# A two-layer graph attention kernel: paired head sums, a two-partition row scan and an extra PE product

## The reference, cut to what matters

```
# layer 0
score = einsum('ehd,ehd->eh', K[src], Q[dst]) / sqrt(32) + edge_bias
m     = segment_max(score, dst)
ex    = exp(score - m[dst]);  denom = segment_sum(ex, dst)
out   = segment_sum(ex / denom[dst] * V[src], dst) @ Wp + bp
# then residual, layer norm, 1024-wide GELU network, layer norm
# layer 1
feat  = (h @ W_lin + b_lin) @ W_gat
e     = leaky_relu(sum(feat*attn_l)[src] + sum(feat*attn_r)[dst], 0.2)
m     = segment_max(e, dst); a = exp(e - m[dst]) / segment_sum(...)
out   = leaky_relu(segment_sum(feat[src] * a, dst) + gat_bias, 0.01) + h_in
```

## Time and profile before

| | |
|---|---|
| time, 3 runs | median 5992.57 us (5990.07 to 6003.05) |
| profiled execution | 5990.54 us, of which the span is 5988.6 |
| busy in the span | PE 91%, PEld 72%, DVE 82%, POOL 63%, ACT 53% |
| mean granted PE clock | 0.896 of 2.4 GHz |
| gathers of layer 0 | start at 369.2, last at 2648.5 us |
| gathers of layer 1 | start at 3660.1, last at 5734.3 us |
| longest shares of the chain that ended last | PE L816 35%, issue 18%, DVE L1199 7%, DVE L1193 7% |

### The profile page before, as it was taken

One profiled execution on the slowest core, in us unless ns is written; L12 is line 12 of the kernel. 1 busy time (PEld: TensorE's weight loads), 2 busy tenths in 40 slices (PEclk: granted clock), 3 DMA queues, 4 the chain that ended last, 5 costly groups with the idle time before them and its releaser, 6 DMA issues.

```text
span 5988.6 us, 127287 instructions
## 1 busy us (share of the span) xinstructions
PE 5460.7 (91%) x26094; PEld 4327.4 (72%) x26094; DVE 4924.3 (82%) x12464; ACT 3152.8 (53%) x10275; POOL 3747.5 (63%) x4022
## 2 busy tenths in 40 slices
PE   8978888888888888888999998999999999999988
PEld 5556666666666666667999996777777777777766
DVE  4469999999999999996777775887888788878864
ACT  3446666666566566643333334555555555655533
POOL 1147776666667666644444446777777777777733
PEclk9999999999999999999999997777777777767789
DMA  5668898888888888872222224777777777777767
GB/s 177 212 222 290 286 290 284 286 287 282 287 283 288 286 284 283 288 234 83 85 85 85 84 83 140 221 218 222 218 220 218 219 218 218 220 218 219 218 201 230
DMA packets 723026, 1313.61 MB, mean 219 GB/s; under 512 B 109088, under 2 KB 502132, under 8 KB 722421
## 3 DMA queue, kind: packets, MB, share of 16 engines
q0 software_dynamic: 200192, 634.41, 36.8%
q1 hardware_dynamic: 444802, 422.18, 23.4%
q10 hardware_dynamic: 77426, 250.73, 10.9%
HBM read 964.16 MB, written 342.73 MB: 218 GB/s over the span
## 4 chain that ended last, share of the span: by engine, by line
PE 37%; DVE 30%; issue 18%; POOL 5%; DMA 4%; DVEq 3%; SPq 2%; ACT 2%; POOLq 1%; ACTq 0%
PE bank L816 35%; DVE sred L1199 7%; DVE prod L1193 7%; DVE ev L1284 5%; DVE acc L1299 4%; POOL Gf L525 3%; DMA Gf<-ft_tab,srcs 3%; PE bank L819 2%; POOL Gf L576 1%; DVE U L1251 1%; DVE Y L1252 1%; DVE scan L1261 1%; DVEq L1181 1%; DVEq L1284 1%; DVE scan L1239 1%
## 5 line engine op out<-in xcount | busy, mean ns | idle before, releaser
L816 PE MATMUL bank<-ev,oh 128*128 128x264 f32 x7040 | 2310.6, 459 | 88.7 <-DVE ev L1284 88.0
L525 POOL DMA_INDIRECT Gf<-kv_tab,srcs x1564 | 1570.4, 1004 | 724.1 <-issue 480.1
L525 POOL DMA_INDIRECT Gf<-ft_tab,srcs x1564 | 1598.9, 1022 | 483.2 <-issue 401.8
L816 PEld LDWEIGHTS bank<-ev,oh 128*128 128x128 f32 x7040 | 1480.0, 223 | 346.0 <-DVE ev L1284 123.4
L816 PE MATMUL bank<-Gf 128*128 128x128 f32 (+3 forms) x6480 | 1263.8, 346 | 22.1 <-ACT Gf L805 15.6
L1284 DVE TENSOR_TENSOR ev<-Gf,ex 128x528 f32<-128x528 f32 x1760 | 1232.9, 701 | 2.1 <-ACT ex L688 1.4
L816 PE MATMUL bank<-qs,oht 128*128 128x256 f32 x3520 | 954.8, 394 | 226.9 <-DVE prod L1193 226.6
L816 PEld LDWEIGHTS bank<-Gf 128*128 128x128 f32 x6480 | 967.2, 192 | 221.0 <-issue 98.5
L621 ACT ACTIVATE absd<-lane,dlocs 128x128 f32<-128x128 f32 x3520 | 1112.9, 389 | 4.0 <-DVE bms L1166 3.5
L816 PEld LDWEIGHTS bank<-qs,oht 128*128 128x128 f32 x3520 | 599.5, 190 | 437.6 <-issue 371.8
L1299 DVE SCALAR_TENSOR_TENSOR acc<-acc,same,bank 128x264 f32<-128x264 f32 x1540 | 736.0, 478 | 34.2 <-PE bank L816 30.8
...
## 6 DMA issues: line engine op xcount, KB each, us to landing
...
qs<-q_tab SPq DMA_DIRECT2D x880, 128.0 KB
qs<-dst_tab SPq DMA_DIRECT2D x880, 128.0 KB
Gf<-sums SPq DMA_DIRECT2D x196, 132.0 KB, 2.1
...
Gf<-in_x SPq DMA_DIRECT2D x196, 128.0 KB, 2.1
Gf<-kv_tab,srcs POOLq DMA_INDIRECT x1564
Gf<-ft_tab,srcs POOLq DMA_INDIRECT x1564
```

The costliest lines, as they stand in the source:

```text
L525: pool.indirect_dma_start(out=rows[layer][:, m % SLOTS[layer], k, :], out_offset=None, in_=tab, in_offset=bass.IndirectOffsetOnAxis(ap=src ...
L816: return nc.tensor.matmul(o, a, r, start=first, stop=end)
```

## The change

1. **Row stage.** Two partitions hold the two directions: partition 0 the row in forward order, partition 1 reversed. PE makes them by products with `ident` and a reversed identity `anti` (four products of 2x128 for three transposes of 1x128). ACT copies two rows for three, DVE makes one scan `uy` over 2x136 for two scans and a subtraction. `columns` becomes four products: two of 8 columns, which yield the difference of both directions on all partitions (with constants `minus_first` and `plus_second`), and two of one column. PE's `rexp` product goes; ACT's `rescale` moves from s=2 to s=4 and works on 128 partitions.
2. **Layer 0, head sums.** `reduce` runs on odd steps only, over two steps at once (128x1024 in, 128x32 out); `prod` has four places for two.
3. **Layer 1, PE.** Every step has one further product of 128x256 in fp32 (`unread`), into a PSUM bank that nothing reads, between `spread` and `agg`.

Left out of the diff: the tiles' memsets and constants in the prologue (each engine waits for two more of POOL's).

```diff
@@ -189,26 +189,29 @@
         oh0 = sb("oh0", [P, 2, 2])
-        prod = sb("prod", [P, 2, 2, D])
+        prod = sb("prod", [P, 4, 2, D])
         absd = sb("absd", [P, 2, 4, P])
...
         ats = sb("ats", [P, P + 1])
-        wa = sb("wa", [P, 1])
+        wa = sb("wa", [P, 3])
         sred = sb("sred", [P, P])
...
         S = sb("S", [P, P])
-        scan1 = sb("scan1", [P, P])
-        scan2 = sb("scan2", [P, P + 1])
-        wlf = sb("wlf", [1, 3, H * RW + 1])
-        U = sb("U", [1, H * RW + 1])
-        Y = sb("Y", [1, H * RW + 1])
-        ct = sb("ct", [1, H])
-        xy = sb("xy", [1, 2, P])
-        rx = sb("rx", [1, H])
-        rexp = sb("rexp", [1, H])
+        scan1_0 = sb("scan1", [P, P + 1])
+        scan1, last_0 = scan1_0[:, 0:P], scan1_0[:, P - 1:P + 1]
+        scan2_0 = sb("scan2", [P, P + 2])
+        scan2, first_0 = scan2_0[:, 1:P + 2], scan2_0[:, 0:2]
+        anti = sb("anti", [P, P])
+        minus_first = sb("minus_first", [2, P])
+        plus_second = sb("plus_second", [2, P])
+        wv = sb("wv", [2, 2, H * RW + 1])
+        uy = sb("uy", [2, H * RW])
+        xy = sb("xy", [2, 2, P])
+        rx = sb("rx", [P, H])
+        rexp = sb("rexp", [P, H])
         rm = sb("rm", [P, 2, H])
...
@@ -647,39 +655,39 @@
             def factors(B):
-                act.wait_ge(E_["r_mm"], B.c + 1)
+                act.wait_ge(E_["r_exp"], B.c + 1)
                 act.wait_ge(E_["oh0_made"], 2 * B.c + 2)
-                act.activation(rm[:, B.par, :], bank[7][:, 392:392 + H], ACT.Identity, scale=oh0[:, B.par, 0:1],
+                act.activation(rm[:, B.par, :], rexp[:, :], ACT.Identity, scale=oh0[:, B.par, 0:1],
                                bias=oh0[:, B.par, 1:2]).then_inc(E_["rm_made"], 1)
             def carried(B):
-                copy(wlf[0:1, 1, 0:H * RW].rearrange("p (h c) -> p h c", c=RW)[:, :, 0],
-                     U[0:1, 0:H * RW].rearrange("p (h c) -> p h c", c=RW)[:, :, CH], E_["carried"])
+                copy(wv[0:1, 1, 0:H * RW].rearrange("p (h c) -> p h c", c=RW)[:, :, 0],
+                     uy[0:1, :].rearrange("p (h c) -> p h c", c=RW)[:, :, CH], E_["carried"])
             def links(B):
                 act.wait_ge(E_["pat"], B.c + 1)
                 act.activation(ats[:, 0:P], bank[7][:, 0:P], ACT.Copy,
-                               accum_out=wa[:, 0:1]).then_inc(E_["ats_made"], 1)
+                               accum_out=wa[:, 1:2]).then_inc(E_["ats_made"], 1)
             def row_values(B):
                 act.wait_ge(E_["rows_mm"], B.c + 1)
-                copy(wlf[0:1, :, 1:].rearrange("p q (h c) -> p q h c", c=RW)[:, :, :, 0:CH],
-                     bank[7][0:1, 0:3 * P].rearrange("p (q h c) -> p q h c", q=3, c=CH), E_["rows_cp"])
+                copy(wv[0:2, :, 1:].rearrange("p q (h c) -> p q h c", c=RW)[:, :, :, 0:CH],
+                     bank[7][0:2, 0:2 * P].rearrange("p (q h c) -> p q h c", q=2, c=CH), E_["rows_cp"])
             def entering(B):
-                act.wait_ge(E_["row"], ROW * B.c + 2)
-                copy(xy[0:1, 0, :].rearrange("p (h c) -> p h c", c=CH),
-                     U[0:1, 0:H * RW].rearrange("p (h c) -> p h c", c=RW)[:, :, 0:CH], E_["xy_cp"])
-                copy(xy[0:1, 1, :].rearrange("p (h c) -> p h c", c=CH),
-                     Y[0:1, 1:].rearrange("p (h c) -> p h c", c=RW)[:, :, 1:RW], E_["xy_cp"])
+                act.wait_ge(E_["row"], B.c + 1)
+                before = uy[0:2, :].rearrange("p (h c) -> p h c", c=RW)[:, :, 0:CH]
+                copy(xy[0:2, 0, :].rearrange("p (h c) -> p h c", c=CH), before, E_["xy_cp"])
+                copy(xy[0:2, 1, :].rearrange("p (h c) -> p h c", c=CH), before[:, ::-1, ::-1], E_["xy_cp"])
             def rescale(B):
-                act.wait_ge(E_["row"], ROW * B.c + 3)
-                act.activation(rx[:, :], ct[:, :], ACT.Relu).then_inc(E_["rx_made"], 1)
+                act.wait_ge(E_["r_mm"], B.c + 1)
+                act.wait_ge(E_["scan_b"], 2 * B.c + 2)
+                act.activation(rx[:, :], bank[7][:, 392:392 + H], ACT.Relu).then_inc(E_["rx_made"], 1)
                 act.wait_ge(E_["rx_made"], B.c + 1)
                 act.activation(rexp[:, :], rx[:, :], ACT.Exp, scale=-1.0).then_inc(E_["r_exp"], 1)
...
@@ -706,9 +714,8 @@
                             row_values(A)
-                        if s == 2 and A.live:
+                        if s == 4 and A.live:
                             rescale(A)
-                        if s == 4 and A.live:
                             factors(A)
...
@@ -902,6 +909,10 @@
                 mm(o, oh[:, B.tri, 2 * s + 1, :], ev[:, s % 4, 1, :], False, True).then_inc(E_["agg"], 1)
+            def unread():
+
+                mm(bank[0][:, 0:D], ident[:, :], w_l[:, 0, :])
+
             def scores_turned(B):
...
@@ -909,23 +920,24 @@
             def row_values(B):
                 pe.wait_ge(E_["scan_a"], 2 * B.c + 2)
-                for q, v in enumerate((wa[:, 0:1], scan1[:, P - 1:P], scan2[:, 0:1])):
-                    m = tr(bank[7][0:1, q * P:(q + 1) * P], v)
+                for q, (ahead, back) in enumerate(((wa[:, 1:3], wa[:, 0:2]), (last_0, first_0))):
+                    mm(bank[7][0:2, q * P:(q + 1) * P], ahead, ident[:, :], True, False)
+                    m = mm(bank[7][0:2, q * P:(q + 1) * P], back, anti[:, :], False, True)
                 m.then_inc(E_["rows_mm"], 1)
             def columns(B):
                 pe.wait_ge(E_["xy_cp"], 2 * B.c + 2)
-                nc.tensor.transpose(bank[7][:, 384:385], xy[0:1, 0, :], ident[0:1, 0:1])
-                nc.tensor.transpose(bank[7][:, 385:386], xy[0:1, 1, :], ident[0:1, 0:1]).then_inc(E_["cols_mm"], 1)
+                mm(bank[7][:, 392:392 + H], minus_first[0:2, :],
+                   uy[0:2, :].rearrange("p (h c) -> p h c", c=RW)[:, :, 0], True, False)
+                mm(bank[7][:, 392:392 + H], plus_second[0:2, :],
+                   uy[0:2, H * RW - 1::-RW], False, True).then_inc(E_["r_mm"], 1)
+                mm(bank[7][:, 384:385], xy[0:2, 0, :], ident[0:2, 0:1])
+                mm(bank[7][:, 385:386], xy[0:2, 1, :], ident[0:2, 1:2]).then_inc(E_["cols_mm"], 1)
             def maxima_turned(B):
                 pe.wait_ge(E_["scan_b"], 2 * B.c + 2)
                 tr(bank[6][:, 2 * P:3 * P], scan2[:, 1:P + 1]).then_inc(E_["m_tr"], 1)
-
-            def rescale(B):
-                pe.wait_ge(E_["r_exp"], B.c + 1)
-                mm(bank[7][:, 392:392 + H], ones[0:1, :], rexp[0:1, :]).then_inc(E_["r_mm"], 1)
             def links_turned(B):
                 pe.wait_ge(E_["arep_made"], B.c + 1)
...
@@ -944,6 +956,8 @@
                             spread(layer, C, r)
+                        if layer == 1 and B.live:
+                            unread()
                         C, r = step_at(B, s - 12)
...
@@ -953,8 +967,6 @@
                             maxima_turned(A)
-                        if s == 3 and A.live:
-                            rescale(A)
                         if s == 5 and B.live:
...
@@ -1051,18 +1064,21 @@
             V = nc.vector
-            dve.wait_ge(S_["const_made"], 8)
+            dve.wait_ge(S_["const_made"], 10)
             dve.wait_ge(S_["setup_loaded"], 32)
             def fresh(ch):
-                ch.did(V.memset(wlf[:, :, :], -BIG))
+                ch.did(V.memset(wv[:, :, :], -BIG))
                 ch.did(V.memset(bank[6][:, 0:1], -BIG))
...
             c0.did(V.memset(ats[:, P:P + 1], 0.0))
+            c0.did(V.memset(wa[:, :], 0.0))
+            c0.did(V.memset(scan1_0[:, P:P + 1], 0.0))
+            c0.did(V.memset(scan2_0[:, 0:1], 0.0))
             for kvo in kvos:
...
@@ -1190,19 +1206,21 @@
                 dve.wait_ge(S_["rows_rdy"], u + 1)
                 dve.wait_ge(E_["qexp"], u + 1)
-                V.tensor_tensor(prod[:, s % 2, :, :], step_rows(0, at)[:, :, 0:D],
+                V.tensor_tensor(prod[:, s % 4, :, :], step_rows(0, at)[:, :, 0:D],
                                 bank[2 + s % 2][:, :].rearrange("p (k n) -> p k n", k=2),
                                 ALU.mult).then_inc(E_["prodd"], 1)
             def reduce(B, s):
+
+                a = s - 1
                 dve.wait_ge(E_["prodd"], B.c * ST + s + 1)
-                V.tensor_reduce(hc(sred[:, :])[:, :, 2 * s:2 * s + 2].rearrange("p h c -> p c h"),
-                                prod[:, s % 2, :, :].rearrange("p k (h w) -> p k h w", h=H), AXX,
+                V.tensor_reduce(hc(sred[:, :])[:, :, 2 * a:2 * a + 4].rearrange("p h c -> p c h"),
+                                prod[:, a % 4:a % 4 + 2, :, :].rearrange("p a k (h w) -> p (a k) h w", h=H), AXX,
                                 ALU.add).then_inc(E_["redd"], 1)
             def scores(layer, B):
                 if layer == 0:
-                    dve.wait_ge(E_["redd"], B.c * ST + ST)
+                    dve.wait_ge(E_["redd"], (B.c + 1) * ST // 2)
                 else:
                     dve.wait_ge(E_["sadd"], 9 * B.n + 9)
...
```

(17 more changed lines are left out.)

20 lines of the change are left out of this document (13 added, 7 removed).

## The result

The changed kernel takes 6062.49 us (median of 4 runs, 6051.45 to 6070.24) against 5994.11 before (5990.07 to 6003.05): ratio 1.0106, 95% interval 1.0093 to 1.0119. It is slower by 68 us. The prediction said 5979, and its range ended at 6030. The profiled execution has a span of 6068.4 us.

| us | up to layer 0 | layer 0 | between | layer 1 | rest | mean gather, layer 0 / 1 |
|---|---|---|---|---|---|---|
| before | 369 | 2279 | 1012 | 2074 | 254 | 1.004 / 1.022 |
| after | 372 | 2342 | 1007 | 2092 | 255 | 1.045 / 1.033 |

A forecast was written before the change was run, and what follows sets the result against it. DVE was taken to bound layer 0 and POOL's gather pace layer 1. Layer 0 +6, layer 1 -17 - 3 and prologue +0.5 took 5990.5 to 5977; 2 us for the median gave 5979, range 5895 to 6030.

The forecast's parts named there:

- +6: Layer 0 in total: a new DVE wait eats the whole saving, so the layer takes 6 us more.
- -17: Layer 1: DVE's work stretches POOL's gathers less, 17 us saved; bounds -117 and +40 us.
- POOL (busy 1371 of 2000 us) and ACT (1210) have room: Layer 0: judged by busy time, POOL and ACT can take the changed work; no cost counted.
- DVE's saving: Layer 0: one scan less saves 0.53 us per block, paired head sums 0.22; together 0.75, 82 us over 110 blocks.
- The wait of `df`: Layer 0: DVE waits 0.80 us per block before df for PE's turned maxima; block 20.92 us against 20.83.
- The double sum: Layer 0: a head sum over two steps holds DVE 1.11 to 1.12 us, saving 0.055 per pair.
- `whole_scans`: Layer 0: it would start at 1.96 us, its columns come at 2.09; 0.13 us, part of the same 0.80 wait.
- clock above 0.95: Layer 1: with six long PE passes a step instead of four, the granted clock rises from 0.72 to above 0.95.
- C: Rival, chance 0.22: slower, layer 0's wait before df on PE's work exceeds the saving; 6029 us if layer 1 gives nothing.
- The signs of error: Forecast wrong if layer 0 blocks fall below 20.5 us, a layer 1 gather waits for a semaphore, or clock stays near 0.7.
- the share of half clock at which PE falls below POOL's pace: Layer 1: PE falls below POOL's 18.86 us a block if the clock is at half for f = 0.24 of the time.
- the lower bound for `columns`: Layer 0 row stage on PE: eight columns passes for two cost at least +0.3 us; +0.76 taken, upper bound +1.0.

The follow-up runs named there:

- e12: Changed kernel, but in layer 0 POOL passes on a landed span after three further spans instead of two; 6003.21 us, ratio 1.0009 to the kernel before.
- e4: Changed kernel with the two 8-column gap products moved from before the xy products to behind the turned maxima; 6010.42 us, ratio 1.0023 to the kernel before.
- e1: Kernel before with the paired (double) head sums of layer 0 alone; 6019.94 us, ratio 1.0034.
- e2: Kernel before with the row stage of the change alone, single head sums, no unread product; 6047.35 us, ratio 1.0079.
- e3: Kernel before with the unread product of layer 1 alone; 5997.33 us, ratio 0.9997.
- e5: Changed kernel with exponentials written to PSUM, two banks for PE's sums instead of three, DVE's add ahead of ev; 5957.53 us, ratio 0.9938 to the kernel before.

## Why the prediction was wrong

The profiled execution took 6070 us where the sum gave 5977. Of these 93 us, 57 are layer 0 (+63 for +6) and 34 the gathers of layer 1 (+17 for -17).

- **The failed step: "POOL (busy 1371 of 2000 us) and ACT (1210) have room".** In layer 1 the prediction added the 0.305 us behind each gather and found POOL's pace; in layer 0 it took busy time for load. The same sum there, 16 x 1.309 = 20.95 us, and 1.9 to 2.7 us of register loads and landing stops (from the kernels in which POOL is never held by the ring) fill 22.9 to 23.6 of the 23.44 us that DVE allows. DVE's block was a bound with another right behind it. That this second bound is what cost layer 0 its 63 us is shown by e12: with four fifths of the landing stops and half of the gap at the loads gone, and DVE's work unchanged, layer 0 takes 2274 us.
- **DVE's saving**: right in kind. With the wait cut nearly by half (e4) the median block is 20.44; e1's fell by 0.20 for 0.22 forecast, e2's by 0.40 for 0.53.
- **The wait of `df`**: right in kind and mis-sized, 0.46 us a block (42.6 over 92) for 0.80, since DVE comes to `df` 4.15 us after the scan (4.61 less 0.46) and not 3.87; `columns` held PE 0.98 (1410.21 to 1411.19) for 0.97. The double sum held DVE 1.13 (1408.01 to 1409.14) for 1.115. The balance came out as said: the undisturbed block is 20.82. `whole_scans` waited 2.7 us in all, forecast clear.
- **What pushed POOL over**: the double sums lengthened its gathers from 1.005 to 1.040 (e1); the row stage left their length in layer 0, but made DVE ask sooner (a block in 20.44), and POOL stopped 72.1 us at landings for 64.9 (e2). There a span lands 3.95 us after its second gather (median) for 3.68; why it lands later was not followed. With both, eight spans take 24.04 us; over 782 spans that is 2350, and layer 0 took 2342.
- **Layer 1**: clock above 0.95 (0.98), gaps of 0.30, POOL bound, all as forecast. The gathers went the other way, 1.022 to 1.033, which is 1564 x 0.011 = 17 us and the measured +17; the forecast took -17 and named +40 as a bound. No row gave the sign. The row stage alone takes the gathers to 1.045 and the layer to 2110 (e2), the unread product alone leaves them at 1.021 (e3), and the later gap products bring them back to 1.023 (e4).
- **Rivals**: C had the right sign with the wrong place: its wait before `df` was shorter than forecast, not longer. No rival had POOL in layer 0. The signs of error that the text named (blocks under 20.5, a gather of layer 1 on a semaphore, clock at 0.7) did not occur; the one that did was not on the list.
- **Slips in the working**, none of which moves the forecast: the share of half clock at which PE falls below POOL's pace comes to 0.23, not 0.24; a double sum of 1.115 us for two of 0.58 saves 0.045 a pair, not 0.055; two transpose passes in 0.21 us are 0.105 each, not 0.07, so the lower bound for `columns` would be +0.6; and 512 + 151 cycles at 0.96 GHz are 0.691 us where the trace has 0.675.

Two cures of layer 0 and one of layer 1 were shown: three spans instead of two (e12, -68 us in layer 0), the later gap products (e4, -37), and exponentials in PSUM (e5, -121 in layer 1). That POOL's register loads can be read ahead of time was not tried.
